# Attention and routed experts on one core: x and output transposed by DMA, x in a ring of five, second attends and scatters moved forward

## The chip, the cores and the metric

The kernel runs on one core of one Trainium2 chip. Five engines work side by side, each through its own instructions in order, and wait for each other on semaphores: TensorE (PE, matmuls), VectorE (DVE), ScalarE (ACT), GpSimd (POOL) and SyncE (SP, which here only issues DMAs). 16 DMA engines move the data. The metric is the device time of one execution in microseconds (us), less is better.

## What is computed

x is [8, 1024, 256] in float32. With a row norm of x, xn, the result is x plus an attention of xn plus a mixture of experts of xn (which itself adds xn):

```
xn = layernorm(x)
Q, K, V = heads(xn@Wq+bq), heads(xn@Wk+bk), heads(xn@Wv+bv)      # 16 heads of 16
Qp, Kp = relu(unit(Q)@proj)+0.1, relu(unit(K)@proj)+0.1          # 64 features, unit: by the vector's norm
out = (Qp @ (Kp.T V)) / (Qp @ sum(Kp)) ; attn = out @ Wo + bo
top 2 of 8 experts per row, capacity 2561, ranks counted over all rows in order
ffn = sum_k gate_k * (silu(xn_row @ w1[e]) @ w2[e]) + xn
result = x + attn + ffn
```

## The kernel before

Every float32 matrix is split into a high and a low float16 part and multiplied in three passes (`PASSES`). The kernel has two stages. **The attention loop** goes over the 8 batches b. One turn (`pe_turn`, `dve_turn`, `act_turn`, `pool_turn`, `sp_turn`, each an order written out by hand for its engine) does the attention of batch b and, woven into it, the preparation ("prep") of batch b+1: the last turn (7) is the "tail" without a preparation. **The expert stage** follows: 71 tiles of 256 gathered rows go through the experts, with POOL's gathers and adding scatters and SP's DMA transposes (`rows_turn`, L429).

A turn, in DVE's order: `choose` (top 2 experts, L1258 MAX8 first); `row_sums(b+1)` (bn_stats L1198, waits for x of batch b+1); `v_over_norm(b, 1)` (L1248 to L1250, waits for POOL's `norm_refine`); `row_factors` (L1206, rsqrt chain); `normalise_rows` (L1216); `place_read`; the copy of the key-value sums kvt (L1385); `q_low` (L1319, low part of the q features); `kv_build`; `constant_part` and four `attend_drain` (L1336) for half 0 of the batch; q_low of half 1; `normalise`, `place` (the slots of each row, L1280 to L1298), `o_low` (L1352); the same for half 1; in between `qk_halves` of b+1 (L1232); `norms` (guess of 1/sqrt, L1238, then POOL refines, L1034 to L1039); `out_drain` (L1363: adds resid).

ACT reads x's high part (`xn_high`), the features (`k_relu` L517, `q_relu` L525), q and k with bias (`qk_read_half`, L505 and L507), v (L547), and makes `resid` (L559) as the last thing of a preparation. SP's `x_load(b+2, half)` waits for `resid_ready` of batch b+1, since resid is made from the same two x buffers. `hi` and `lo` parts of xn and of the attention's output are turned on PE (`x_transpose` L718, `o_transpose` L833; 8 transposes a bank) and copied out of PSUM by ACT (L543, L578). POOL makes low parts (`x_low`, `w_low`), refines norms in 13 steps and scatters 16 sets of 128 records per batch into the slot table (`scatter`, L1046): eight after the last attend, then `norm_refine`, then eight. Each turn also splits one expert's weights (`w_load`, `w_high`, `w_low`, `w_store`). Three small PSUM banks go round in the order of `BODY`: each user waits until the user three before has been read.

## Time and profile before

| | us |
|---|---|
| median of 3 runs | 1437.63 (1431.65 to 1439.33) |
| the profiled execution | 1448.41 |
| its span, first to last instruction | 1446.8 |
| attention loop with its start | about 677 |
| expert stage | about 770 |
| mean granted TensorE clock | 0.912 |

Over the span PE is busy 86%, DVE 55%, ACT 46%, POOL 55%. In a timeline each row is a start, a duration, the engine, the line and the operation with what it writes and reads; in brackets stands how long the engine sat idle before and what released it. "remote" there is a release that the profile can't name. A line with "SPq" is the issue of a DMA.

### The profile page before, as it was taken

How to read it: one execution, taken by the hardware profiler on the slowest of the kernel's cores; microseconds unless marked ns; L12 is line 12 of the kernel's file. 1: busy time of each engine (PE TensorE's matmuls, PEld its weight loads, DVE VectorE, ACT ScalarE, POOL GpSimd, SP SyncE). 2: the span in 40 equal slices, each digit the busy share in tenths (PEclk: the TensorE clock that was granted, in tenths of full speed). 3: DMA queues.
4: the chain of work that ended last, by engine and by line, in shares of the span. 5: the costliest groups of instructions: out<-in, count | busy, mean ns of one | idle time of the engine just before them, and what ended most of it. 6: DMA issues, size and time to landing. Idle time of an engine off the chain costs nothing.

```text
span 1446.8 us, 38172 instructions
## 1 busy us (share of the span) xinstructions
PE 1250.6 (86%) x14334; PEld 997.8 (69%) x14334; DVE 792.5 (55%) x1830; ACT 663.7 (46%) x1140; POOL 802.3 (55%) x804
## 2 busy tenths in 40 slices
PE   4886877878796968644999999999999999999997
PEld 2555554545555545423888888888888888888886
DVE  6676858586767677653433434344444434344442
ACT  3766766666766666631323323232323333232322
POOL 3637382846556473861256656555555556565553
PEclk9798787979797978856999999999999999999999
DMA  2223232322413232504864444444544444344451
GB/s 84 98 73 111 89 118 89 118 89 75 132 45 118 89 105 66 182 25 154 275 180 82 78 77 70 75 75 74 78 75 74 77 77 77 69 77 75 78 78 15
DMA packets 156139, 133.73 MB, mean 92 GB/s; under 512 B 93825, under 2 KB 144258, under 8 KB 154946
## 3 DMA queue, kind: packets, MB, share of 16 engines
q1 hardware_dynamic: 122338, 95.58, 23.2%
q0 software_dynamic: 33632, 35.71, 15.3%
q8 instruction: 129, 2.11, 0.6%
q14 instruction: 40, 0.33, 0.1%
HBM read 61.83 MB, written 52.61 MB: 79 GB/s over the span
## 4 chain that ended last, share of the span: by engine, by line
PE 58%; DVE 18%; issue 7%; DMA 5%; ACT 5%; POOL 5%; SPq 1%; another core or an unknown queue 1%; ACTq 0%; DVEq 0%; POOLq 0%
PE bank L944 26%; PE bank L960 25%; DVE area L1319 4%; DMA area<-in_x_dram 4%; POOL slot_table L1046 2%; DVE area L1198 2%; DVE area L1216 1%; ACT area L559 1%; PE bank L821 1%; DVE area L1187 1%; PE bank L807 1%; ACT area L578 1%; PE bank L728 1%; PE bank L705 1%
## 5 line engine op out<-in xcount | busy, mean ns | idle before, releaser
L944 PE MATMUL bank<-area 128*128 128x256 f16 x3408 | 385.5, 273 | 20.0 <-DMA area<-xg 15.3
L960 PE MATMUL bank<-area 128*128 x3408 | 383.5, 273 | 0.0
L944 PEld LDWEIGHTS bank<-area 128*128 x3408 | 334.1, 98 | 60.4 <-issue 21.1
L1142 POOL DMA_INDIRECT out_dram<-area,mt x142 | 229.6, 1617 | 251.3 <-ACT area L647 221.8
L1468 DVE TENSOR_SCALAR area<-area 128x512 f16<-128x512 f32 x284 | 129.0, 454 | 422.0 <-ACT area L637 390.0
L960 PEld LDWEIGHTS bank<-area 128*128 128x128 f16 x3408 | 333.3, 98 | 38.7
L637 ACT ACTIVATE area<-bank 128x512 f32<-128x512 f32 x284 | 169.6, 598 | 189.3 <-PE bank L944 176.0
L1046 POOL DMA_INDIRECT slot_table<-area x128 | 128.2, 1001 | 149.3 <-PE bank L821 107.3
L647 ACT ACTIVATE area<-bank,mt 128x256 f32<-128x256 f32 x142 | 59.6, 470 | 329.5 <-PE bank L960 324.8
L1470 DVE SCALAR_TENSOR_TENSOR area<-area 128x512 f16<-128x512 f32 x284 | 196.9, 693 | 9.8
L1135 POOL DMA_INDIRECT xg<-xn_split,mt x142 | 143.5, 1010 | 44.7 <-issue 42.7
L765 PE MATMUL bank<-p_hl,area 32*128 32x128 f16 x1536 | 67.8, 258 | 44.9 <-issue 35.2
L1127 POOL DMA_DIRECT2D mt<-slot_table x71 | 54.3, 765 | 77.1 <-issue 77.1
L705 PE MATMUL bank<-area,w_hl 128*128 128x512 f16 x384 | 95.1, 409 | 1.3 <-ACT area L543 1.3
L765 PEld LDWEIGHTS bank<-p_hl,area 32*128 32x128 f16 x1536 | 55.4, 114 | 55.7 <-issue 45.8
L1319 DVE SCALAR_TENSOR_TENSOR area<-bank,area 128x512 f16<-128x512 f32 x128 | 79.5, 682 | 21.1 <-ACT area L525 20.8
L807 PE MATMUL bank<-area,p_hl 32*128 32x512 f16 x384 | 55.6, 497 | 35.5 <-DVE area L1319 35.5
L525 ACT ACTIVATE area<-bank 128x512 f16<-128x512 f32 x128 | 67.6, 598 | 39.8 <-PE bank L807 22.9
L1007 POOL TENSOR_TENSOR area<-area 128x1024 f16<-128x1024 f32 x16 | 35.4, 2211 | 83.9 <-ACT area L537 83.9
L705 PEld LDWEIGHTS bank<-area,w_hl 128*128 128x128 f16 x384 | 40.1, 105 | 50.3 <-issue 14.0
L1002 POOL TENSOR_TENSOR area<-area 128x1024 f16<-128x1024 f32 x32 | 68.0, 2127 | 0.3 <-ACT area L498 0.2
L505 ACT ACTIVATE area<-bank,bqk_w 128x512 f32<-128x512 f32 x64 | 45.4, 709 | 41.1 <-PE bank L705 41.1
(172 smaller groups left out, 1457.7 us busy)
## 6 DMA issues: line engine op xcount, KB each, us to landing
area<-in_w_dram SPq DMA_DIRECT2D x32, 512.0 KB, 5.3
experts_split<-area SPq DMA_DIRECT2D x32, 512.0 KB, 4.3
area<-experts_split SPq DMA_DIRECT2D x8, 2048.0 KB, 8.1
area<-in_x_dram SPq DMA_DIRECT2D x16, 512.0 KB, 6.8
xn_split<-area SPq DMA_DIRECT2D x16, 512.0 KB, 3.0
out_dram<-area SPq DMA_DIRECT2D x32, 256.0 KB
xg<-xn_split,mt POOLq DMA_INDIRECT x142
area<-xg SPq DMA_TRANSPOSE x142
```

Of the source, the lines that this page charges most:

```text
L637: nc.scalar.activation(h32[j].rearrange("p a b -> p (a b)"), big[j][:, :], ACT.Silu, scale=1.0 / R_SCALE).then_inc(mh_silu, 1)
L705: mm = nc.tensor.matmul(big[n][:, :], w_hl[:, wl, k, c0:c0 + P], xT[half][:, xl * KC + k, :], start=(i == 0 and k == 0), stop=(i == 2 and ...
L765: mm = nc.tensor.matmul(big[j][:, c:c + P], k_hl[g // 2][rows_, m, kl, tok:tok + P], p_hl[rows_, pl, m, j * P:(j + 1) * P], start=(i == 0) ...
L807: mm = nc.tensor.matmul(big[j][:, :], p_hl[rows_, pl, m, j * P:(j + 1) * P], q_hl[half][rows_, m, ql, :], start=(i == 0), stop=(i == 2))
L944: mm = nc.tensor.matmul(big[j][:, i2 * TS:(i2 + 1) * TS], we[:, bass.ds(e * EXPERT + (k * 2048 + wl * 1024 + c * P), P)], moe_xT[t % XT][: ...
L960: mm = nc.tensor.matmul(yb[:, a * D:(a + 1) * D], hT[u % 2][:, c, hl, a * P:(a + 1) * P], we[:, bass.ds(e * EXPERT + off, D)], start=(c == ...
L1046: nc.gpsimd.indirect_dma_start(meta, bass.IndirectOffsetOnAxis(slot_i[:, k, t:t + 1], 0), rec[:, k, t, :], None).then_inc(meta_stored, 16)
L1135: nc.gpsimd.indirect_dma_start(xg[:, t % XR, a, :], None, xs, bass.IndirectOffsetOnAxis(mt[:, u % GRP, a, 0:1], 0)).then_inc(rows_in[t % X ...
L1142: nc.gpsimd.indirect_dma_start(orows, bass.IndirectOffsetOnAxis(mt[:, u % GRP, a, 0:1], 0), y_sb[u % 2][:, a, :], None, bounds_check=last_ ...
L1319: v.scalar_tensor_tensor(rq[:, p_, 1, :], big[n % BIG_BANKS][:, :], 0.0, rq[:, p_, 0, :], ALU.max, ALU.subtract).then_inc(qf_split, 1)
L1468: v.tensor_scalar(hT[u % 2][:, 2 * j:2 * j + 2, 0, :], h32[j], H_SCALE, None, ALU.mult).then_inc(mh_step, 1)
L1470: v.scalar_tensor_tensor(hT[u % 2][:, 2 * j:2 * j + 2, 1, :], h32[j], H_SCALE, hT[u % 2][:, 2 * j:2 * j + 2, 0, :], ALU.mult, ALU.subtract ...
```

## The change

- `resid` goes; the rows are overwritten in place (`resid_rows`), in a ring of five half batches of x (`x_in(b, half)`). `x_load(b+2, 0)` is first in `sp_turn`, `x_load(b+2, 1)` waits until out1 of batch b is drained.
- `row_sums` and `row_factors` of batch b+2 are made in turn b, between `out_drain(b, 0)` and `out_drain(b, 1)`.
- xn and the output are transposed by DMA from SP (`x_turn`, `o_turn`, four of [128, 512] float16 each), behind the store and the load of weights; PE's transposes and ACT's copies go. PE and ACT wait for `x_turned` and `o_turned`.
- The second attends come right after the q features of half 1; `place` follows them on DVE, and the 16 scatters go in one piece. nd has two buffers.
- The norms of half 0 are refined on DVE in place of POOL.

The diff, cut to its core:

```diff
 XR = 4
+HALVES = 5
...
-BODY = (attn("rank", "vsum", "kvT") + prep("xT0", "xT1") + attn("cn", "ab0", "ab1", "ab2", "ab3") + prep("xT2", "xT3")
-        + attn("oT0", "oT1", "ab4", "ab5", "ab6", "ab7") + prep("v0", "v1", "nrm0", "v2", "nrmT0", "v3")
-        + attn("out0", "out1", "oT2", "oT3") + prep("v4", "v5") + attn("out2", "out3") + prep("v6", "nrm1", "v7", "nrmT1"))
+BODY = (attn("rank", "vsum", "kvT", "cn", "ab0", "ab1", "ab2", "ab3", "ab4", "ab5", "ab6", "ab7")
+        + prep("v0", "v1", "nrm0", "v2", "nrmT0", "v3") + attn("out0", "out1") + prep("v4", "v5") + attn("out2", "out3")
+        + prep("v6", "nrm1", "v7", "nrmT1"))
...
-        x_in = [view([HT, D], F32) for _ in range(2)]
+        x_half = [view([HT, D], F32) for _ in range(HALVES)]
...
-        resid = view([NT, D], F32)
...
-        nd = view([HT, H, HD + 1], F32)
+        nd = [view([HT, H, HD + 1], F32) for _ in range(2)]
...
+        def x_in(b, half):
+
+            return x_half[(2 * b + half) % HALVES]
...
-            src = xrows[bass.ds(b * S + half * HS, HS), :].rearrange("(t p) d -> p t d", p=P)
-            hold(sp, resid_ready, (b - 1) * 2 + half + 1)
-            sp.dma_start(x_in[half], src).then_inc(x_loaded[half], 16)
+            src = xrows[b * S + half * HS:b * S + half * HS + HS, :].rearrange("(t p) d -> p t d", p=P)
+            n = 2 * b + half - HALVES
+            if n >= 0:
+                wait_read(sp, "attn", f"out{2 * (n % 2) + 1}", n // 2)
+            if b > 0:
+                sp.wait_ge(x_loaded[half], b * 16)
+            sp.dma_start(x_in(b, half), src).then_inc(x_loaded[half], 16)
+
+        def x_turn(sp, b, half):
+
+            if b > 0:
+                sp.wait_ge(prep_filled, nth("prep", f"v{half * HT + HT - 1}", b - 1))
+            sp.wait_ge(xl_split, b * 2 + half + 1)
+            for t in range(HT):
+                sp.dma_start_transpose(xT[half][:, :, t * P:(t + 1) * P],
+                                       xhl[half][:, t].rearrange("p h n -> p (h n)")).then_inc(x_turned[half], 16)
+
+        def o_turn(sp, b, half):
+
+            if half == 1:
+                sp.wait_ge(attn_filled, nth("attn", "out1", b))
+            elif b > 0:
+                sp.wait_ge(attn_filled, nth("attn", "out3", b - 1))
+            sp.wait_ge(o_split, b * 2 + half + 1)
+            for t in range(HT):
+                sp.dma_start_transpose(oT[:, t], o_hl[:, t].rearrange("p h n -> p (h n)")).then_inc(o_turned[half], 16)
 
         def xs_store(sp, b, half):
...
         def sp_turn(sp, b, phase, x_next=True):
             body = phase == "body"
-            if body:
-                xs_store(sp, b + 1, 0)
+            if body and x_next:
+                x_load(sp, b + 2, 0)
             w_store(sp, b, 0)
             w_load(sp, b, 2)
             if body:
-                xs_store(sp, b + 1, 1)
+                x_turn(sp, b + 1, 0)
+                xs_store(sp, b + 1, 0)
             w_store(sp, b, 1)
             w_load(sp, b, 3)
+            if body:
+                x_turn(sp, b + 1, 1)
+                xs_store(sp, b + 1, 1)
+            o_turn(sp, b, 0)
+            w_store(sp, b, 2)
+            if body:
+                w_load(sp, b + 1, 0)
             out_store(sp, b, 0)
+            o_turn(sp, b, 1)
             out_store(sp, b, 1)
-            w_store(sp, b, 2)
-            if body:
-                w_load(sp, b + 1, 0)
             if body and x_next:
-                x_load(sp, b + 2, 0)
+                x_load(sp, b + 2, 1)
             out_store(sp, b, 2)
             out_store(sp, b, 3)
-            if body and x_next:
-                x_load(sp, b + 2, 1)
             w_store(sp, b, 3)
...
             sp.wait_ge(consts_ready, 1)
             for half in range(2):
+                x_load(sp, 1, half)
                 xs_store(sp, 0, half)
-                x_load(sp, 1, half)
                 w_load(sp, 0, half)
...
         def resid_rows(act, b, half):
 
             act.wait_ge(resid_scales, b * 2 + 2)
-            if b > 0:
-                wait_read(act, "attn", f"out{2 * half + 1}", b - 1)
+            x_rows = x_in(b, half)
             for t in range(HT):
                 n = half * HT + t
-                ins = nc.scalar.activation(resid[:, n, :], x_in[half][:, t, :], ACT.Identity, bias=shift[:, n:n + 1],
+                ins = nc.scalar.activation(x_rows[:, t, :], x_rows[:, t, :], ACT.Identity, bias=shift[:, n:n + 1],
                                            scale=grow[:, n:n + 1])
             ins.then_inc(resid_ready, 1)
...
             act.wait_ge(o_ready, b * 2 + half + 1)
-            nc.scalar.copy(o_hl.rearrange("p t l (h d) -> p l t h d", h=H)[:, 0], nd[:, :, :, 0:HD]).then_inc(o_high, 1)
-
-        def oT_copy(act, phase, b, half):
-            for j in range(2):
-                src = f16(take(act, phase, "attn", f"oT{2 * half + j}", b)).rearrange("p (t c q) -> p t c q", t=2, c=4)
-                nc.scalar.copy(oT[:, 2 * j:2 * j + 2], src).then_inc(attn_taken, 1)
+            if half == 1:
+                act.wait_ge(o_turned[0], (b + 1) * 16 * HT)
+            elif b > 0:
+                act.wait_ge(o_turned[1], b * 16 * HT)
+            nc.scalar.copy(o_hl.rearrange("p t l (h d) -> p l t h d", h=H)[:, 0], nd[half][:, :, :, 0:HD]).then_inc(o_high, 1)
...
             q_relu(act, b, 1)
             if body:
-                xT_copy(act, phase, b + 1, 1)
-                qk_read_half(act, b + 1, 0, 0, 1)
+                qk_read_half(act, b + 1, 0, 0, 2)
             o_hi(act, b, 0)
-            if body:
-                qk_read_half(act, b + 1, 0, 1, 2)
-            oT_copy(act, phase, b, 0)
             if body:
                 qk_read_half(act, b + 1, 0, 2, 4)
                 v_copy(act, phase, b + 1, 0)
                 v_copy(act, phase, b + 1, 1)
                 squares_copy(act, phase, b + 1, 0)
                 v_copy(act, phase, b + 1, 2)
+                v_copy(act, phase, b + 1, 3)
             o_hi(act, b, 1)
             if body:
-                v_copy(act, phase, b + 1, 3)
-            if body:
+                resid_rows(act, b + 1, 0)
+                qk_read_half(act, b + 1, 1, 0, 4)
                 w_high(act, b, 3)
-                qk_read_half(act, b + 1, 1, 0, 2)
-            oT_copy(act, phase, b, 1)
+                resid_rows(act, b + 1, 1)
             if body:
                 v_copy(act, phase, b + 1, HT)
                 v_copy(act, phase, b + 1, HT + 1)
-                qk_read_half(act, b + 1, 1, 2, 4)
                 last_copies(act, phase, b + 1)
...
             q_features(pe, b, 1, 1)
-            if body:
-                x_transpose(pe, phase, b + 1, 1)
-                qk_project(pe, b + 1, 0, False)
-            o_transpose(pe, phase, b, 0)
             for t in range(HT, NT):
                 attend(pe, phase, b, t)
             if body:
+                qk_project(pe, b + 1, 0, False)
                 v_and_squares(pe, phase, b + 1, 0)
+            if body:
+                qk_project(pe, b + 1, 1, False)
             o_project(pe, phase, b, 0)
-            if body:
-                qk_project(pe, b + 1, 1, False)
-            o_transpose(pe, phase, b, 1)
             if body:
                 v_and_squares(pe, phase, b + 1, 1, attended=b)
...
             w_low(pool, b, 2)
-            pool.wait_ge(attn_filled, nth("attn", f"ab{NT - 1}", b))
-            scatter(pool, b, 0, 8)
-            norm_refine(pool, b + 1, 0)
-            scatter(pool, b, 8, 16)
+            scatter(pool, b)
             w_low(pool, b, 3)
             norm_refine(pool, b + 1, 1)
             v_total(pool, b + 1)
...
-            rsqrt_guess(chp, ny, nsq, nu, ready=norm_guess)
+            if half == 1:
+                rsqrt_guess(chp, ny, nsq, nu, ready=norm_guess)
+                return
+            rsqrt_guess(chp, ny, nsq, nu)
+            for step in range(3):
+                chp.link(v.tensor_tensor(nu, nsq, ny, ALU.mult))
+                chp.link(v.scalar_tensor_tensor(ny, nu, -0.5, ny, ALU.mult, ALU.mult) if step == 2 else
+                         v.scalar_tensor_tensor(nu, nu, -0.5, ny, ALU.mult, ALU.mult))
+                chp.link(v.scalar_tensor_tensor(ny, ny, 1.5, nu, ALU.add, ALU.mult) if step == 2 else
+                         v.scalar_tensor_tensor(ny, nu, 1.5, ny, ALU.add, ALU.mult))
+            chp.link(v.tensor_scalar(norm[:, 0], ny, 1e-8 * W_SCALE, None, ALU.add))
...
         def dve_turn(dve, b, phase, first=False):
             body = phase == "body"
-            cha.start(dve, b)
             choose(dve, b)
-            if body:
-                chp.start(dve, b + 1)
-                row_sums(dve, b + 1)
             if not body:
                 place_read(dve, phase, b)
                 place(dve, b, first)
             v_over_norm(dve, b, 1, cha)
             if body:
-                row_factors(dve)
                 normalise_rows(dve, b + 1, 0)
-            if body:
                 place_read(dve, phase, b)
             else:
                 tile_table(dve)
@@ -1391,32 +1375,32 @@
             constant_part(dve, b, 0)
             for t in range(HT):
                 attend_drain(dve, phase, b, t)
-            q_low(dve, b, 1, 0, PAIRS)
-            normalise(dve, b, 0)
-            if body:
-                place(dve, b, first)
-                qk_halves(dve, b + 1, 0, 0, 1)
-            o_low(dve, b, 0)
+            q_low(dve, b, 1, 0, 4)
             constant_part(dve, b, 1)
+            q_low(dve, b, 1, 4, PAIRS)
             for t in range(HT, NT):
                 attend_drain(dve, phase, b, t)
             if body:
-                qk_halves(dve, b + 1, 0, 1, 4)
+                place(dve, b, first)
+            normalise(dve, b, 0)
+            if body:
+                qk_halves(dve, b + 1, 0, 0, 2)
+            o_low(dve, b, 0)
             normalise(dve, b, 1)
             if body:
+                qk_halves(dve, b + 1, 0, 2, 4)
                 norms(dve, phase, b + 1, 0)
+                v_over_norm(dve, b + 1, 0, chp)
             o_low(dve, b, 1)
+            if body:
+                qk_halves(dve, b + 1, 1, 0, 4)
             out_drain(dve, phase, b, 0, first)
-            if body:
-                qk_halves(dve, b + 1, 1, 0, 2)
-                v_over_norm(dve, b + 1, 0, chp)
-                qk_halves(dve, b + 1, 1, 2, 3)
+            if body and b + 2 < B:
+                row_sums(dve, b + 2)
+                row_factors(dve, b + 2)
             out_drain(dve, phase, b, 1, first)
             if body:
-                qk_halves(dve, b + 1, 1, 3, 4)
                 norms(dve, phase, b + 1, 1)
-                chp.end()
-            cha.end()
...
-            for half in range(2):
-                qk_halves(dve, 0, half)
-                if half == 1:
-                    v_over_norm(dve, 0, 0, chp)
-                norms(dve, "first", 0, half)
-            chp.end()
+            qk_halves(dve, 0, 0)
+            norms(dve, "first", 0, 0)
+            v_over_norm(dve, 0, 0, chp)
+            qk_halves(dve, 0, 1)
+            norms(dve, "first", 0, 1)
+            row_sums(dve, 1)
+            row_factors(dve, 1)
```

Beside it `row_sums(1)` and `row_factors(1)` stand ahead of the first turn, `row_factors` waits for `resid_ready` of the batch before, `xn_high` waits for `x_turned`, PE's `o_project` waits for `o_turned`, and `bo_row`, `bo_hl` and `vtmp` share other buffers.

## Rows read from the trace of the kernel before

**Rows 1.** Windows by stage: us; per engine busy us (xinstructions); PEclk, DMA share, GB/s
```profile
199.00:277.00 78.00, 62.89 (x940) 41.12 (x938) 56.73 (x153) 53.69 (x89) 45.77 (x54) 0.82 0.31 96
720.00:1440.00 720.00, 713.47 (x6533) 638.65 (x6530) 309.75 (x540) 218.69 (x407) 406.85 (x337) 1.00 0.45 79
```

**Rows 2.** Timeline of DVE, turn 2: start, us, engine, line, operation [idle before]
```profile
119.88 0.64 DVE L1258 MAX8 area<-area 128x8 f32<-128x8 f32 x8
...
198.19 0.64 DVE L1258 MAX8 area<-area 128x8 f32<-128x8 f32 x8
...
207.84 2.71 DVE L1198 BATCH_NORM_STATS2 area<-area 128x6 f32<-128x256 f32 x8 [2.89 <-DMA area<-in_x_dram]
...
264.12 0.69 DVE L1363 SCALAR_TENSOR_TENSOR area<-bank,area 128x512 f32<-128x512 f32 x1 [0.83 <-remote]
...
276.48 0.64 DVE L1258 MAX8 area<-area 128x8 f32<-128x8 f32 x8
```

**Rows 3.** Timeline of SP's queue, turn 2: issues of DMAs
```profile
200.97 0.38 SPq L386 DMA_DIRECT2D area<-in_x_dram  x1
```

**Rows 4.** Timeline of ACT, turn 2
```profile
203.32 2.06 ACT L517 ACTIVATE area<-bank 128x512 f32<-128x512 f32 x4 [2.38 <-remote]
...
223.03 2.06 ACT L525 ACTIVATE area<-bank 128x512 f16<-128x512 f32 x4
```

**Rows 5.** Timeline of PE, turn 2 and tail turn
```profile
218.90 0.65 PE L790 MATMUL bank<-xg,area 128*32 128x64 f32 x32
...
274.86 0.63 PE L744 MATMUL bank<-ident,area 128*128 128x128 f32 x4
...
613.64 1.93 PE L790 MATMUL bank<-area 128*32 128x64 f32 x64 [6.40 <-DVE area L1250]
```

**Rows 6.** Windows of one engine alone, DVE four times, then POOL
```profile
221.96:264.81 42.85, 33.05 (x75) 0.80 0.24 80
243.22:246.14 2.92, 2.54 (x17) 1.00 0.00 0
6.16:12.16 6.00, 5.52 (x31) 1.00 0.69 195
269.72:271.56 1.84, 1.80 (x4) 1.00 0.01 1
...
203.86:210.97 7.11, 6.04 (x16) 0.65 0.77 261
```

**Rows 7.** Groups by line in turn 2: busy us, mean ns, idle before
```profile
L578 ACT COPY area<-bank 128x1024 f16<-128x1024 f16 x4 | 3.9, 1028 | 2.0 <-PE bank L833 2.0
...
L1280 DVE TENSOR_TENSOR area<-area 128x128 f32<-128x128 f32 x1 | 0.3, 285 | 0.0
```

**Rows 8.** Transposes of the expert stage: by line, SP's timeline, a window of half a us
```profile
L429 SPq DMA_TRANSPOSE area<-xg x142: 1189/1262/2782, 677.6 to 1412.5; - x142
...
802.21 2.50 SPq L429 DMA_TRANSPOSE area<-xg  x2
...
805.00:805.50 0.50, 0.50 (x7) 0.44 (x6) 0.00 (x0) 0.50 (x1) 0.50 (x1) 1.00 0.79 156
```

**Rows 9.** Landing times: L386's loads of x, page part 6, chain of waits
```profile
DMA to landing us min/median/max: 6.5/6.8/8.1
...
xn_split<-area SPq DMA_DIRECT2D x16, 512.0 KB, 3.0
...
1.44 4.62 DMA area<-in_x_dram
```

**Rows 10.** Timelines around scatters: POOL and DVE in turn 2, PE in the tail
```profile
261.55 0.96 POOL L1046 DMA_INDIRECT slot_table<-area  x1 [0.30 <-issue]
...
262.60 0.69 DVE L1363 SCALAR_TENSOR_TENSOR area<-bank,area 128x512 f32<-128x512 f32 x1 [3.58 <-remote]
...
629.29 0.23 PE L821 MATMUL bank<-area 128*128 128x34 f16 x2 [1.23 <-issue]
...
640.67 0.66 PE L821 MATMUL bank<-area 128*128 128x34 f16 x17 [1.23 <-issue]
```

More of the change, by code:

```diff
@@ L289, in moe_attention @@
         xn_ready = sem("xn_ready")
+        x_turned = [sem(f"x_turned{i}") for i in range(2)]
         xs_stored = [sem(f"xs_stored{i}") for i in range(2)]
@@ L315, in moe_attention @@
         o_split = sem("o_split")
+        o_turned = [sem(f"o_turned{i}") for i in range(2)]
         out_stored = [sem(f"out_stored{i}") for i in range(2)]
@@ L452, in _ @@
             sp.dma_start(xs[N:N + P, :], zero_rows).then_inc(zero_stored, 16)
+            for half in range(2):
+                x_turn(sp, 0, half)
             sp.wait_ge(consts_ready, 1)
             for half in range(2):
+                x_load(sp, 1, half)
                 xs_store(sp, 0, half)
-                x_load(sp, 1, half)
                 w_load(sp, 0, half)
@@ L668, in _ @@
             last_copies(act, "first", 0)
+            for half in range(2):
+                resid_rows(act, 0, half)
             act_turn(act, 0, "body", first=True)
@@ L823, in attend @@
             mm.then_inc(attn_filled, 1)
-        def o_transpose(pe, phase, b, half):
-            for j in range(2):
-                dst = f16(small_ap(phase, "attn", f"oT{2 * half + j}", b, pe)).rearrange("p (t c q) -> p t c q", t=2, c=4)
-                if j == 0:
-                    pe.wait_ge(o_split, b * 2 + half + 1)
-                for tl in range(2):
-                    for hl in range(2):
-                        for m in range(KC):
-                            mm = nc.tensor.transpose(dst[:, tl, hl * KC + m, :],
-                                                     o_hl[:, 2 * j + tl, hl, m * P:(m + 1) * P], ident16[:, :])
-                mm.then_inc(attn_filled, 1)
         def o_project(pe, phase, b, half):
@@ L1021, in norm_refine @@
             g = nc.gpsimd
-            steps = [(b * 2 + half) * 13]
+            steps = [b * 13]
             def link(ins, apart=False):
@@ L1030, in link @@
                     pool.wait_ge(pool_norm, steps[0])
-            hold(pool, norm_guess, b * 2 + half + 1)
+            hold(pool, norm_guess, b + 1)
             for _ in range(3):
@@ L1039, in norm_refine, with scatter @@
             g.tensor_scalar(norm[:, half], nu, 1e-8 * W_SCALE, None, ALU.add).then_inc(norm_ready, 1)
-        def scatter(pool, b, n0=0, n1=TOPK * NT):
+        def scatter(pool, b):
             pool.wait_ge(slots_ready, b + 1)
-            for n in range(n0, n1):
+            for n in range(TOPK * NT):
                 k, t = n // NT, n % NT
@@ L1197, in row_sums, with row_factors @@
             for t in range(NT):
-                chp.step(v.bn_stats(bn[:, t, :], x_in[t // HT][:, t % HT, :]))
-            hold(dve, dve_prep, chp.base + chp.n)
+                chp.step(v.bn_stats(bn[:, t, :], x_in(b, t // HT)[:, t % HT, :]))
+            chp.wait()
             for t in range(NT):
                 chp.step(v.bn_aggr(mv[:, t, :], bn[:, t, :]))
-        def row_factors(dve):
+        def row_factors(dve, b):
             chp.wait()
             chp.link(v.tensor_scalar(va, mv[:, :, 1], 1e-5, None, ALU.add))
+            if b > 0:
+                dve.wait_ge(resid_ready, b * 2)
             rsqrt(chp, vy, va, vu)
```

94 lines of the change are left out of this document (33 added, 61 removed).

## The prediction, made before the changed kernel was run

> **What bounds the kernel now.** I read the stage table first [rows 1]. TensorE (PE) is busy in 713.5 of 720 us of the expert stage, which the change doesn't touch; in a turn of the attention loop no engine is full (PE 62.9, VectorE (DVE) 56.7, ScalarE (ACT) 53.7, GpSimd (POOL) 45.8 of 78 us). So a turn is bound by a chain of hand-offs, and I looked next at what DVE does in one [rows 2]. A turn runs from one `choose` (MAX8, 198.19) to the next (276.48): 78.3 us. I write times in a turn as c+t, c being that start. DVE waits 2.9 us for the DMA of x, at c+9.6 it begins the statistics; v over norm, row factors and the first rows follow, and it copies the key-value sums (L1385) only at c+23.8 [rows 6]. The load of x was issued at 200.97, since SyncE's queue (SP) had waited until ACT had written resid [rows 3]. ACT's first k relu starts at c+5.1, its first q relu at c+24.8, after rows that DVE normalised late [rows 4], though PE had ended its sums at 219.55, c+21.4 [rows 5]. Then comes DVE's long stretch to the end of the drain of out1, 264.81, c+66.6; and 11.7 us from there to the next choose [rows 2].
>
> **The front of a turn.** The change loads x and makes its statistics a turn ahead, and takes resid off the turn's last place on ACT. So ACT can begin its k relus at about c+0.1. From that relu to PE's last sum it was 203.32 to 219.55, 16.2 us [rows 4, 5]. v over norm of half 1 needs POOL's 13 steps, 7.1 us [rows 6], which now start at c (POOL's scatters are over by then, below); with its own work of 1.8 and a copy held up behind POOL it ends near c+10.3, and PE wants it at about c+12. I put L1385 at c+16.2 (bounds 15.5 and 17.5): a gain of 7.6 us. This is all that the early x gives.
>
> **The transposes.** Removed per turn: 64 transposes on PE and 8 copies on ACT of 1.02 us [rows 7]. The x ones lay beside DVE's q splits: no gain. For o, PE's first bank and ACT's two copies were the path, about 2.7 us (0.6+2x1.03) from o_low to oT. Added are 16 transposes on SP. The expert stage shows the same [128x512] f16 form: 142 of them, 1.19 to 2.78 us of SP each, a pair in 2.50, and the data of a pair's second moving until about 805.5, 2.0 us after its issue at 803.5 [rows 8]. So a half of four holds SP 5.0 us and is there 3.75+2.1 = 5.9 us after its first issue. The same rows bound SP's part by 4.8 (4 at 1.19) and 11 us (4 at 2.78); I take the pair, which is two in a row. Against 2.7 us that is 3.2 later for o, and **whatever stands behind them in SP's queue waits 5 us more**.
> The Trainium skill (Advanced Engine Details and Errata, section X-Bar Transpose (TRN2)) says that transposing DMAs on this chip are as fast as regular ones. The rows disagree for this form: a 512 KB store lands in 3.0 us [rows 9], a transposed half in 5.9. What the rule would give is one of the rivals.
>
> **From L1385 to out1's drain.** DVE was busy in 33.05 of 42.85 us of this stretch [rows 6]; 4.4 of the rest were late signals for the two drains of out (one in rows 10). New in it: ten links of norm refinement, taken from POOL, on 128x128 elements, nearest row L1280 with 0.285 [rows 7], so with hand-offs 3.1 us; v over norm of half 0, 1.8 [rows 6], and two qk halves of about 0.74, which stood behind out1's drain before. That is 39.5 us of work, some 41 with the hundredths between chained steps. The waits come from a ladder, in which each step starts when its engine and its inputs are free (durations as in before): q relus 16, attend drains 0 to 3 end 28.8, q splits of half 1 with constant part 1 in their gap end 34.4, PE's second attends and their drains 38.1, place (2.9 [rows 6]) 41.0, normalise 0 43.0, two qk halves, o_low 0 45.7. SP transposes o half 0 until 51.6; only then may ACT overwrite o_hl (52.7), write resid half 0 (2.0 us) and read q and k of half 1 in 4 pairs of 1.3 us, until 59.9. DVE meanwhile has qk halves, normalise 1, norms, refinement, v over norm until 55.8, o_low 1 57.0; its last qk half waits for ACT, 60.6, and out1 is drained at c+62.0, where it was c+66.6. So 45.8 us, and 4.6 us of the gain are left here.
>
> **From there to the next choose.** This term decides. `x_load(b+2,1)` takes the ring's buffer that out1's drain frees, and stands on SP behind `o_turn(b,1)` and a store; `row_sums(b+2)` stands on DVE right behind that drain and ahead of `out_drain(b,1)`. So: SP's store of out0 61.75, four transposes 66.7, a store 67.1, the x load. It lands 4.6 us later at the least (the chain's first load, from 1.44) or 6.8 (median of 14, 6.5 to 8.1) [rows 9]; I take 5.5, nearer the first, since little else is in flight: 72.6. Statistics and row factors, 6.0 us where POOL is still [rows 6]: 78.6. out2 drained 79.3. PE's square sums wait for exactly that bank (three small banks in turn): 1.06, ACT's copy 0.6, the transpose 0.63 (rows 5 has the last), DVE's 0.8, with 0.2 of hand-offs: choose at **c+82.6**, against 78.3. POOL's 16 scatters at 1.27 run from 41.0 to 61.3, under cover. PE idles from about 72 on. **A wait chain of 20.6 us stands where 11.7 stood.**
>
> **Sum.** Five turns (1 to 5) of +4.3: +21.5. The first: PE's first projection waits 5.9 us for four transposes instead of about 3 (+3); statistics of batch 1 (6.0) now stand ahead of the first choose and hold up the gates and v over norm: out1 near 112.8 instead of 108.2, the next choose at 112.8+20.6 = 133.3 instead of 119.9 [rows 2]: +13.4. Turn 6 has no statistics: o half 1 is there at 67.6, out2 drained 70.1, choose 75.4: -2.9. Tail turn: PE's wait of 6.4 us for v over norm [rows 5] and some 2 us of late relus go, -8.4; two o halves with 3.2 more each, less what the earlier attends give back, +5.4: -3.0. Together +29 us. Against the profiled execution, 1448.4, that is 1477; it lies 10.8 above the median of the runs shown, and I set the difference on the median: 1437.6+29 = **1466.6 us**. Every bound low: a turn of 77.0 (no idle on DVE beyond its 41, load 4.6), first turn +8, turn 6 -8, tail -8: -14.5, 1423. Every bound high: a turn of 86.6 (load 6.8, transposes at 1.5, front 17.5): +60, 1498.
>
> **Rivals.** (1) Not slower: the ladder is too pessimistic, and DVE runs from L1385 to out1 with little idle. It decides where front, stretch and tail sum below 78.3, so at a stretch under 42.3 us with the load at 4.7 (mine is 45.8); halfway the sum is about 1437, at the end 1423. For it: DVE's work alone allows it, and a wait of known length stands only at the load. Against it: in the trace DVE idles 9.8 us in this stretch [rows 6], and o_hl adds a wait. Chance 0.22. A variant: four transposes take SP and the DMA engines no longer than one plain DMA of 512 KB (0.38 on SP [rows 3], 3.0 to land [rows 9]); SP would be free 4.6 us earlier, the turn 78.0 and the sum about 1434; 142 rows speak against it, 0.02. It is what the page named above would give.
> (2) Much slower: signals freeze while POOL issues scatters. In the trace DVE's drain of out0 starts as POOL's eighth scatter in a row ends, 3.6 us after DVE was free; and in the tail turn, under 16 in a row, PE's attends come one or two per 1.2 us until 640.67, then 17 at once [rows 10]. The change puts 16 in a row into every turn, c+41 to c+61, over square sums, norms, and q and k of half 1. If nrmT0, due at 48.9, reaches DVE only at 61.3, about 11.7 us later, each of seven turns grows by as much: 1466.6+82 = 1549. Against it: the tail's freeze alone is some 12 us and the runs without a recording are 10.8 shorter, as if the freeze were the recording's. 0.18, partial freezes included.
> The Trainium skill (SBUF — State Buffer, section SBUF: two separate sides, the box on the "DVE blocks DMA" trap) warns that DVE work on the port it shares with GpSimd keeps POOL from writing descriptors, and refinement now runs on DVE during scatters. The rows don't show it: scatters keep 0.96+0.30 us beside DVE's work [rows 10], so nothing is charged.
> (3) My forecast, slower by 12 to 60 us: 0.58.
>
> **Chances.** A difference within 0.5% (7 us) is what a measurement can't tell from none. Rival 1 with its variant (0.24) split into faster 0.10 and same 0.14; slower is 0.76. The range leaves out most of rival 2 and the low end of rival 1: 1430 to 1512.
>
> **What would show it.** In the changed kernel: DVE waiting 8 to 11 us per turn at bn_stats for the DMA of x, with PE idle beside the end of it; the copy of the key-value sums near c+16; out1 drained near c+62; on SP four transposes of 1.25 us ahead of the x load. A DVE wait of 5 us or more for nrmT0 would be rival 2. I am wrong if the statistics start without a wait, or if a turn takes 78 us or less.

## The result and the profile after

The changed kernel takes 1497.11 us (median of 4, 1496.20 to 1500.55) against 1438.07 us (4 runs, 1431.65 to 1439.33) for before: ratio 1.0427, interval 1.0403 to 1.0450, slower by 59 us where 29 were forecast. Its profiled execution took 1496.2 us, span 1494.5.

Windows of after: turn 2, turn 6 (which has no statistics), the expert stage; columns as in [rows 1]:

```profile
219.16:302.54 83.38, 56.03 (x863) 34.27 (x858) 59.15 (x164) 46.48 (x81) 41.37 (x39) 0.80 0.43 117
...
560.03:641.92 81.89, 56.86 (x885) 34.10 (x879) 53.77 (x134) 46.47 (x81) 41.66 (x39) 0.79 0.43 102
...
772.00:1494.00 722.00, 711.33 (x6511) 636.57 (x6509) 307.17 (x536) 218.08 (x406) 404.79 (x336) 1.00 0.45 78
```

The expert stage takes 761.2 us from its first matmul on, for 760.4. PE does less in a turn (56.0 us against 62.9 [rows 1]), yet a turn is 5 us longer. Timeline of DVE, turn 2 of after, the lines that answer to [rows 2]:

```profile
219.16 0.64 DVE L1249 MAX8 area<-area 128x8 f32<-128x8 f32 x8
...
234.74 0.41 DVE L1369 COPY area<-bank 128x256 f32<-128x256 f32 x1
...
280.54 1.28 DVE L1353 SCALAR_TENSOR_TENSOR area<-bank,area 128x512 f32<-128x512 f32 x2
...
291.68 2.71 DVE L1176 BATCH_NORM_STATS2 area<-area 128x6 f32<-128x256 f32 x8 [9.86 <-DMA area<-in_x_dram]
...
297.67 1.28 DVE L1353 SCALAR_TENSOR_TENSOR area<-bank,area 128x512 f32<-128x512 f32 x2
...
301.81 0.29 DVE L1218 COPY area<-bank 128x128 f32<-128x128 f32 x1 [2.86 <-PE bank L747]
```

The copy of the key-value sums stands at c+15.6 (before: c+23.8), out1 is drained at c+62.7, and then DVE does nothing for 9.9 us. SyncE's queue says what it waits for:

```profile
265.73 5.13 SPq L414 DMA_TRANSPOSE area<-area  x4
...
281.25 0.39 SPq L424 DMA_DIRECT2D out_dram<-area  x1
281.74 5.14 SPq L414 DMA_TRANSPOSE area<-area  x4
286.92 0.58 SPq L424 DMA_DIRECT2D out_dram<-area  x1
287.60 0.41 SPq L395 DMA_DIRECT2D area<-in_x_dram  x1
```

Store, four transposes, store, then the load of x at c+68.4, which lands 4.1 us later. PE in the same stretch:

```profile
288.23 0.58 PE L835 MATMUL bank<-area 2*128 2x512 f16 x1 [6.10 <-DMA area<-area]
288.74 2.74 PE L839 MATMUL bank<-wo_hl,area 128*128 128x256 f16 x12
...
298.41 1.08 PE L740 MATMUL bank<-area,hsel 128*32 128x512 f32 x8 [4.05 <-DVE area L1353]
```

It waits for the transposed o half, 6.5 us behind its first issue, and then for DVE's drain of out2. The same twelve matmuls took 1.48 us before; windows of PE alone, first after, during DVE's wait, then before, from out1's drain to choose:

```profile
281.82:291.68 9.86, 3.76 (x17) 0.52 0.61 160
```
```profile
264.81:276.48 11.67, 10.44 (x114) 1.00 0.36 120
```

The granted clock is 1.00 up to about c+63, where PE's six matmuls end that stand between a wait of 2.6 us and one of 6.1, and 0.50 (the level of 1.2 GHz) from c+64 to c+73, so also for the twelve matmuls of 2.74 us. Over the window that makes 0.52. In before's window, with PE busy in 10.4 of 11.7 us, it stays at 1.00.

Turns are 79.6, 82.8, 83.4, 85.2, 86.8, 85.6 and 81.9 us. They differ mostly by when o half 0 is transposed. ACT's second o_hi, which waits for it, in turns 2 and 4, and SP's four issues in turn 4:

```profile
272.21 1.04 ACT L602 CAST area<-area 128x1024 f16<-128x1024 f32 x1 [2.46 <-DMA area<-area]
...
443.59 1.04 ACT L602 CAST area<-area 128x1024 f16<-128x1024 f32 x1 [5.37 <-DMA area<-area]
```
```profile
434.22 6.96 SPq L414 DMA_TRANSPOSE area<-area  x4
```

From first issue to landing: 6.5 us in turn 2, 9.4 in turn 4, where out1's drain ends at c+65.5 instead of c+62.7. GpSimd's 16 scatters run beside it, from c+42 to c+63.

### The profile page after: what moved, and what is told of

Its sections match the earlier page's. It is cut to its first block, busy times and chain, and to the rows that moved or that the text cites. A ratio compares the mean times of both kernels' runs of the same rounds, so it can differ in the third digit from the quotient of the medians.

```text
span 1494.5 us, 37183 instructions
## 1 busy us (share of the span) xinstructions
PE 1221.0 (82%) x13822; PEld 958.3 (64%) x13822; DVE 819.8 (55%) x1910; ACT 605.0 (40%) x1076; POOL 762.5 (51%) x690
## 4 chain that ended last, share of the span: by engine, by line
PE 52%; DMA 2%; DVE 1%; issue 1%; SPq 1%; POOL 0%; ACT 0%; POOLq 0%
PE bank L930 25%; PE bank L946 25%; DMA area<-experts_split 1%; PE bank L839 1%; SPq L414 1%; DMA area<-area 1%; PE bank L810 0%; PE bank L824 0%; PE bank L793 0%; POOL out_dram L1120 0%; DVE area L1310 0%; PE bank L835 0%; DVE area L1241 0%; DMA experts_split<-area 0%; DMA out_dram<-area,mt 0%
## 5 line engine op out<-in xcount | busy, mean ns | idle before, releaser
L946 PEld LDWEIGHTS bank<-area 128*128 128x128 f16 x3408 | 333.4, 98 | 38.8 <-issue 0.2
L1030 POOL DMA_INDIRECT slot_table<-area x128 | 138.1, 1079 | 123.0 <-DVE dump_f L1289 80.3
L664 ACT ACTIVATE area<-bank,mt 128x256 f32<-128x256 f32 x142 | 59.6, 471 | 329.5 <-PE bank L946 329.5
L1105 POOL DMA_DIRECT2D mt<-slot_table x71 | 54.0, 761 | 76.2 <-issue 76.2
L1018 POOL TENSOR_TENSOR area<-area 128x128 f32<-128x128 f32 x24 | 11.0, 456 | 147.0 <-DVE area L1155 145.8
L721 PEld LDWEIGHTS bank<-area,w_hl 128*128 128x128 f16 x384 | 39.2, 104 | 72.2 <-issue 35.6
L731 PE MATMUL bank<-w_hl,area 128*128 128x264 f16 x384 | 58.1, 297 | 26.5 <-DVE area L1353 26.5
L824 PEld LDWEIGHTS bank<-area 128*128 128x128 f16 x1536 | 45.2, 106 | 51.0 <-issue 33.9
L824 PE MATMUL bank<-area 128*128 128x34 f16 x1536 | 47.3, 191 | 31.8 <-issue 22.9
L731 PEld LDWEIGHTS bank<-w_hl,area 128*128 128x128 f16 x384 | 37.6, 103 | 53.3 <-DVE area L1353 31.0
```

The lines of the kernel that those rows point to most:

```text
L721: mm = nc.tensor.matmul(big[n][:, :], w_hl[:, wl, k, c0:c0 + P], xT[half][:, xl * KC + k, :], start=(i == 0 and k == 0), stop=(i == 2 and ...
L731: mm = nc.tensor.matmul(dst[:, 0:D + E], xT[half][:, xl * KC + k, tl * P:(tl + 1) * P], w_hl[:, wl, k, 2 * D:], start=(i == 0 and k == 0), ...
L824: mm = nc.tensor.matmul(dst[:, p_ * KVW:(p_ + 1) * KVW], rq[:, p_, rl, tl * P:(tl + 1) * P], kv_hl[:, kl, p_, :], start=(i == 0), stop=(i ...
L946: mm = nc.tensor.matmul(yb[:, a * D:(a + 1) * D], hT[u % 2][:, c, hl, a * P:(a + 1) * P], we[:, bass.ds(e * EXPERT + off, D)], start=(c == ...
L1030: nc.gpsimd.indirect_dma_start(meta, bass.IndirectOffsetOnAxis(slot_i[:, k, t:t + 1], 0), rec[:, k, t, :], None).then_inc(meta_stored, 16)
```

## The experiments

The chips on which these ran differ, so ratios to before on the same chip are given. DMA transposes are in none of these kernels. The expert stage's are plain copies of the same tiles, and those of a turn are stood in for by plain copies (**copies**) or made by PE as before (**on PE**). So the price of the transposing DMA itself is bracketed, not measured apart. The plain copies leave out the turning: the experts, and where the turn has copies too also q, k, v and the routing, work on unturned rows, with the same numbers of matmuls, copies and bytes. c is a turn's choose, as in the prediction.

**1. The control, and how the time of a turn follows the queue.** In before, `dma_start_transpose(moe_xT..., xg...)` became `dma_start`.

> The kernel before with the expert stage's 142 transposing DMAs made plain copies of the same tiles (what is left out: the turning of the gathered rows; the experts multiply unturned rows). Every other kernel of the study has this too. It is the control for it: TensorE bounds that stage (713.5 of 720 us busy), so every theory expects the time of before, 1438 us, within 5 us, and turns of the attention loop of 78.3 us.

1432.3 us, ratio 0.9960 (0.9945 to 0.9975); turns of 78.4 us. Of the 5 us less, 3.2 lie in the expert stage (757.2 for 760.4 us in the profiles).

Then after, with one or three copies for each transpose (the three move a half, a quarter and a quarter of the tile):

```
-  sp.dma_start_transpose(oT[:, t], o_hl[:, t]...)
+  for c0, c1 in O_PARTS: sp.dma_start(oT[:, t, c0:c1], src[:, c0:c1])     (x the same)
```

> The kernel after with each of its 16 transposing DMAs a turn replaced by three plain copies that together move the same [128x512] f16 tile (left out: the turning of x and o, so q, k, v and the routing are made from unturned rows; the counts of matmuls, copies and bytes are the same). Three issues of about 0.42 us with gaps of 0.05 hold SyncE's queue 5.6 us for a half where four transposes held it 5.1. Theory (what the transposes cost is their time in the queue and the landing behind it): 1497 us within 8, with the wait of 9 to 10.5 us for x at bn_stats and turns of 82 to 87 us. Rival (it is the transposing itself, by the DMA engines' own work, that stretches everything else): 1480 us or less.

1530.8 us, ratio 1.0645 (1.0627 to 1.0662): both sides missed, since twelve issues hold SP longer than I had reckoned. SP, then DVE, in turn 2:

```profile
296.36 7.55 SPq L419 DMA_DIRECT2D area<-area  x12
303.95 0.59 SPq L429 DMA_DIRECT2D out_dram<-area  x1
304.64 0.41 SPq L397 DMA_DIRECT2D area<-in_x_dram  x1
```
```profile
308.79 2.71 DVE L1181 BATCH_NORM_STATS2 area<-area 128x6 f32<-128x256 f32 x8 [12.35 <-DMA area<-in_x_dram]
```

> As the kernel with three copies, but one plain copy for each transposing DMA: a half of four holds SyncE's queue 1.9 us. My forecast's variant said 1434 us for this. With the measured turns of 84.7 us: x is loaded 3.5 us earlier at the turn's end, the second o_hi of ScalarE comes 3 us earlier and out1's drain 1 to 2.5 us, so turns of 79 to 80 us and 1460 us, 1450 to 1467. Rival (the statistics' wait stays whatever the queue does, since out1's drain frees the buffer at c+62): 1475 or more. Rival (transposes are the whole loss): 1440 or less.

1458.7 us, ratio 1.0134 (1.0107 to 1.0160), as expected from after's turns. SP is held for 2.40 us, DVE waits 8.67:

```profile
272.00 2.40 SPq L419 DMA_DIRECT2D area<-area  x4
```
```profile
280.75 2.71 DVE L1181 BATCH_NORM_STATS2 area<-area 128x6 f32<-128x256 f32 x8 [8.67 <-DMA area<-in_x_dram]
```

Means of turns 1 to 5 against SP's hold by a half of o: 80.9 us at 2.4, 84.7 at 5.1 (after), 89.4 at 7.6. That is 1.4 and 1.9 us of turn for one of queue: a half in the queue is paid behind out1's drain, and the other one partly before it, through ACT's o_hi. A line between the two kernels of plain copies gives 85.3 at 5.1 us (an estimate), so after's transposes cost about what plain copies with their hold would.

**2. Both transposes on PE**, with ident16, the banks and ACT's copies of before; ring, statistics, attends and scatters as in after.

> The kernel after with both transposes back on TensorE and their copies on ScalarE, as in before, and the expert stage's 142 transposing DMAs made plain copies (left out: the turning of the gathered rows). What is left of the change is the ring of five, the early statistics, the early second attends and the 16 scatters in a row. Theory (ring and order are sound, the DMA transposes and what they do to SyncE's queue cost all): the load of x goes out as out1 is drained, near c+61, lands at c+65.5, statistics until c+71.5, out2 drained c+72, choose c+76: turns of 76 to 77 us, the first +5, turn 6 and the tail -10 together: 1423 us, 1415 to 1435. Rival (statistics between the two drains cost even with a free queue, because x still lands 4.4 us after the drain that frees its buffer): turns of 79 us or more, 1440 or more.

1443.5 us, ratio 1.0056 (1.0039 to 1.0073); against the control, 11 us slower (14 by the two ratios). The rival won, my theory missed by 20 us. Turn 2:

```profile
275.18 1.28 DVE L1379 SCALAR_TENSOR_TENSOR area<-bank,area 128x512 f32<-128x512 f32 x2
...
281.93 2.71 DVE L1202 BATCH_NORM_STATS2 area<-area 128x6 f32<-128x256 f32 x8 [5.47 <-DMA area<-in_x_dram]
```

With an empty queue DVE still waits, since the buffer is freed by the very drain that stands ahead of the statistics; turn 2 has the shortest of these waits, in turns 1 to 5 they are 5.5 to 8.2 us, 6.7 on average. Turns with them take 80.0 us, turn 6 without takes 72.8 (74.4 when the same kernel ran again). Against the control this kernel is at 1.0056/0.9960 = 1.010; what is left to after's 1.0427 is a factor of 1.033, and that is what transposing by DMA costs over transposing on PE.

**3. Take the wait away.** `HALVES = 6`, and both `x_load(b+2)` at the head of `sp_turn`; statistics stay. It ran twice, on two chips, the second time beside its base.

> The kernel with the transposes on TensorE (turned_by_pe: 1443.5 us, turns of 80.0), with six half buffers in the ring and both loads of batch b+2 at the head of turn b. Theory (what is lost against before is the wait for the load of x, 5.5 us of DVE in each turn with statistics): bn_stats starts as out1 is drained, c+62.5, ends with the factors c+68.5, out2 and out3 drained at c+70.5, choose at c+74.6: six turns of 5.4 us less, 1411 us, 1405 to 1420. Rival (statistics between the two drains cost by their own 6 us, wherever x is: turn 6 without them took 72.8): 1425 to 1435. Rival (the DMAs moved to the head of the turn get in the way there): 1438 or more.

> The kernel with both transposes on TensorE once more, on one chip with the three below. On the chip where before takes 1437 us and no wait is put down as remote it was 1443.5 (ratio 1.0056). If this chip is like that, the same ratio. If it is like the other one (before 1445 us, remote waits of 3 to 5 us for PE's and DVE's signals until the last of 16 scatters has gone at c+64): out1 is drained at c+66 instead of c+62 and the tail turn is 13 us or more longer, 1443.5 + 6*3 + 15 = 1475 us, ratio about 1.02.

> Ring of six and both loads of x at the head of the turn, transposes on TensorE. Theory (the wait of 5.5 us for x goes): 25 to 32 us less than turned_by_pe_2 on the same chip, whichever chip it is. Rival (DMAs or the statistics' own 6 us hold the end): within 8 us of it.

On the first chip (before: 1445 us) it took 1457.1 us, ratio 1.0080 (1.0049 to 1.0111): the theory's range is missed, and the last rival's, in which this lies, is met for another reason (below). On the second (before: 1436) the base took 1445.7 (1.0055, 1.0036 to 1.0074) and this 1410.5, ratio 0.9821 (0.9804 to 0.9838), the 1411 expected, and 35 us below its base where 25 to 32 were: the wait that goes is longer than the 5.5 us reckoned with. It is 1.4% below the control, whose expert stage has plain copies too, so it beats before as well as after. There, turn 4, DVE goes on without a wait, and the turn takes 73.6 us (turns 1 to 5: 74.4 on average):

```profile
411.49 1.28 DVE L1379 SCALAR_TENSOR_TENSOR area<-bank,area 128x512 f32<-128x512 f32 x2
412.69 2.70 DVE L1202 BATCH_NORM_STATS2 area<-area 128x6 f32<-128x256 f32 x8
```

On the first chip, the same turn, DVE between the drains of out0 and out1 and ACT before the copy of o's transposed half 1:

```profile
432.69 0.69 DVE L1379 SCALAR_TENSOR_TENSOR area<-bank,area 128x512 f32<-128x512 f32 x1 [3.43 <-remote]
```
```profile
432.78 1.93 ACT L585 COPY area<-bank 128x1024 f16<-128x1024 f16 x2 [4.90 <-remote]
```

Both wait until c+65.6, as GpSimd's last scatter (issued at c+63.4) has gone. Such waits for a remote signal stood in the profile of before too [rows 10], and in none of after, of the control or of the other kernels on chips where before takes 1436 to 1438 us. Their place is that of my rival 2. Four kernels ran on that chip, all with such waits, and the same four elsewhere without any: so whether they come depends on the chip. On which chip the profile of before was taken isn't on record; its 1448.4 us lies among the 1441 to 1449 that before takes on this one. What after would take there isn't known.

**4. Only the order in SP's queue.** One copy for each transpose, `x_load(b+2,1)` ahead of `o_turn(b,1)`.

> The kernel with one plain copy for each transposing DMA, and x_load(b+2,1) ahead of o_turn(b,1) in SyncE's queue. Theory (each us that the load of x waits in the queue is a us of the turn): the load goes out at c+61.5 instead of c+64.2, bn_stats starts at c+67 instead of c+69.8, and the copies of o half 1, 0.5 us later, still land before the statistics end at c+73: 2.5 us less in each of six turns, 1443 us, 1440 to 1448. Rival (o half 1, now behind the load, becomes the bound): 1455 or more.

> One plain copy for each transposing DMA, once more. Where no remote waits stand 1458.7 (ratio 1.0134); on a chip with them 3 to 4 us more in each turn and 15 in the tail, 1495 us, ratio 1.035.

> The same with x_load(b+2,1) ahead of o_turn(b,1). Theory (each us of the load's wait in the queue is a us of the turn): 10 to 16 us less than one_copy_for_one_2 on the same chip. Rival (o half 1, which now waits for out1's drain as well, takes the load's place as the bound): within 5 us of it. The first look had it 24 us above one_copy_for_one, but on another chip; if that is the edit and not the chip, it is again 15 us or more above.

The first run was on the chip with remote waits and gave 1482.8 us, ratio 1.0257 (1.0224 to 1.0289). On the other: base 1458.7 (1.0151, 1.0133 to 1.0168), edit 1440.9, ratio 1.0051 (1.0022 to 1.0079): inside the first range, and somewhat more than the 10 to 16 us of the second. 18 us for two lines exchanged: the load goes out at c+60.8 instead of c+63.8, and DVE waits 5.44 instead of 8.5:

```profile
267.32 0.38 SPq L397 DMA_DIRECT2D area<-in_x_dram  x1
267.80 2.48 SPq L419 DMA_DIRECT2D area<-area  x4
```
```profile
272.73 2.71 DVE L1181 BATCH_NORM_STATS2 area<-area 128x6 f32<-128x256 f32 x8 [5.44 <-DMA area<-in_x_dram]
```

**5. The wait away, the queue still slow.** Three copies, ring of six, loads at the head of the turn.

> The kernel with three plain copies for each transposing DMA (1530.8 us, ratio 1.0645; turns of 89.4, DVE waits 12.3 us for x), with the ring of six and both loads of x at the head of the turn. Theory (with so slow a queue, o half 1 is the next bound, so only part of the wait comes back): the statistics end at c+72, PE still gets o half 1 at c+74.5, so the turn ends as its turn 6 without statistics, 84.6: six turns of 4.7 us less, 1503 us, ratio 1.045 (1.040 to 1.050). Rival (the wait comes back whole, 12 us a turn): 1460 us or less.

1503.3 us, ratio 1.0479 (1.0452 to 1.0506). DVE's 12.35 us of waiting are gone, but turns fall only from 89.4 to 84.6: the next bound is o half 1, as PE's projection ends:

```profile
288.43 2.70 DVE L1180 BATCH_NORM_STATS2 area<-area 128x6 f32<-128x256 f32 x8
...
300.66 0.69 DVE L1357 SCALAR_TENSOR_TENSOR area<-bank,area 128x512 f32<-128x512 f32 x1 [6.17 <-PE bank L843]
```

By the same reading the wait of 9.9 us in after is worth what turn 6 shows, 84.7-81.9 = 2.8 us; but there out1 is drained at c+65.8, in turns 1 to 5 at c+63.8 on average, so it may be up to 4.8. Both are estimates, no run took the wait out of after. The 9.1 us from turn 6 to the 72.8 of turn 6 on PE (7.5 to its second run) are the transposes'.

**6. The statistics elsewhere**: `row_sums`, `row_factors` behind the next turn's choose; transposes on PE, ring of five.

> The kernel with the transposes on TensorE and row_sums and row_factors taken from between the drains and put right behind the next turn's choose. There DVE waits 4.1 us for GpSimd (v over norm), so 6 us of statistics push the copy of the key-value sums from c+15.6 to c+17.6 to c+19. Theory: the end of a turn is that of turn 6, so a turn takes 72.8+2 to 3.5 = 75 to 76.3 us against 80.0, six of them: 1415 to 1425 us. Rival (DVE's work is the bound, so it does not matter where the statistics stand): 1438 or more.

> The kernel with the transposes on TensorE and the statistics behind the next turn's choose, once more. Its first look showed the row factors, chained operations on [128x8], taking 1.1 to 2.3 us each beside GpSimd's norm refinement where they take 0.17 to 0.31 alone, and the copy of the key-value sums at c+22 instead of c+15.6. Theory: a turn is that of turn 6 without statistics and 6.4 us more, 72.8+6.4 = 79.2 against 80.0: on a chip without remote waits 1438 us, ratio 1.002 (0.999 to 1.005); with them 1485 again, ratio 1.027.

1485.1 us, ratio 1.0269 (1.0234 to 1.0303), on the chip with remote waits; 1435.3, ratio 0.9990 (0.9974 to 1.0005), on the other. Turns take 78.3 us: the first expectation, 75 to 76.3, failed, and only 8 us are gained on the base; the second, 1438 us, holds within 3 us. The place was free only in name. DVE, then GpSimd beside it, operations of DVE that take 0.17 us between the drains:

```profile
210.24 2.30 DVE L1191 TENSOR_TENSOR area<-area 128x8 f32<-128x8 f32 x1
...
214.76 2.04 DVE L1193 SCALAR_TENSOR_TENSOR area<-area 128x8 f32<-128x8 f32 x1
...
224.42 0.42 DVE L1398 COPY area<-bank 128x256 f32<-128x256 f32 x1 [1.95 <-PE bank L798]
```
```profile
209.64 0.54 POOL L1047 TENSOR_SCALAR area<-area 128x128 f32<-128x128 f32 x1
210.16 2.35 POOL L1020 TENSOR_TENSOR area<-area 128x1024 f32<-128x1024 f32 x1
...
214.66 2.12 POOL L1010 TENSOR_TENSOR area<-area 128x1024 f16<-128x1024 f32 x1
```

The expectation put this down to the norm refinement. The rows say otherwise: the refinement ends at 210.2 (L1047 is its last step), and DVE's operations on [128x8] beside it take 0.17 to 0.23 us. The two slow ones start just after a large subtraction or addition of GpSimd (`v_total`, L1020, and `w_low`, L1010) and end with it, 212.54 for 212.51 and 216.80 for 216.78. The key-value sums are copied at c+21.5 instead of c+15.6.

**7. Two scatters instead of 16** in each turn but the last, one copy for each transpose.

> The kernel with one plain copy for each transposing DMA (1458.7 us, turns of 80.9) with 2 of 16 scatters in each turn but the last (left out too: 14 of 16 stores of a turn into the slot table). Theory (16 scatters in a row cost next to nothing): 1454 to 1460 us; of single waits only that of ScalarE's second o_hi in turn 6 (4.9 us) goes. Rival (scatters hold up signals or the transfers beside them in every turn): 3 us or more less a turn, 1438 or less.

> One plain copy for each transposing DMA, 2 of 16 scatters in each turn but the last, once more (base: 1458.7 us, ratio 1.0134 and 1.0151). Its first look had turns of 79.1 against 80.9 and 73.7 against 78.9 in turn 6, but a tail turn of 108 us with all 16 scatters on the chip with remote waits. Theory: without such waits the tail is 86 us again, so 5*1.8+5 = 14 us less than the base: 1444 us, ratio 1.004 (1.001 to 1.007). Rival (scatters cost nothing where nothing is put down as remote): ratio 1.011 or more.

On the chip with remote waits 1465.6 us, ratio 1.0141 (1.0111 to 1.0172). Its turns are those of the other chip, 79.1 us, with no remote wait before the tail, so there it is the row of scatters that brings the waits. Its tail takes 108 us for 87.6. Under the tail's 16 scatters (619.3 to 639.3) DVE's copy of the key-value sums waits 16.6 us, and under the expert stage's first eight gathers (from 660.3) PE's attends crawl from 660.30 to 671.64 as in [rows 10]:

```profile
642.01 0.42 DVE L1375 COPY area<-bank 128x256 f32<-128x256 f32 x1 [16.64 <-remote]
```

On the other chip 1443.9, ratio 1.0066 (1.0044 to 1.0087): the first expectation (scatters cost next to nothing) fails, the second holds, with turns of 79.1 for 80.9 and 73.9 for 78.9. The load of x lands 4.3 instead of 5.5 us after its issue, and ACT's wait for the first half in turn 6 goes. So 14 scatters more a turn cost 15 us there in all (10 to 12 by the ratios) with no signal held up; what shows is that DMAs beside them land later.

## Why the prediction was wrong, step by step

**What bounds, and the sign: right.** The term called decisive was: out1 drained c+62.0, load issued 67.1, statistics at 72.6, choose 82.6; turn 2 shows 62.7, 68.4, 72.5 and 83.4. The 72.5 is in part luck: the load goes out 1.3 us late and lands 1.4 us sooner than reckoned. And turn 2 is the second shortest of turns 1 to 5, which take 84.7 on average. The front (15.6 to 16.4, forecast 16.2) is right.

**Wrong by 30 us** are four terms of the sum: turns 1 to 5 by 10.6, turn 6 by 4.8, the first turn by 3.1, the tail and what it was compared with by 11.3. 1497 lies in the range, but near its upper end.

1. *Turns 1 to 5*: +32.1, forecast +21.5. "So a half of four holds SP 5.0 us and is there ... 5.9 us after its first issue": the hold is 5.13, the landing 6.5 to 9.4. It was read from pairs of the expert stage; here half 1, issued as the last scatters go, lands in 6.5 us each time, and half 0, beside the scatters, in 6.5 to 9.4. ACT's second o_hi starts at c+53.0 to c+55.9 instead of 51.6, and from the copy of the key-value sums to the end of out1's drain it is 48.0 us on average, not 45.8. Experiment 7 shows the scatters' part, on copies. From out1's drain to the issue of the load it is 5.8 us instead of 5.1, and from the start of out2's drain to choose 5.1 on average instead of 4.0: PE's lower clock, with 1.1 to 1.9 us for the square sums, up to 1.50 for 0.85 for v's six matmuls behind them (not in my chain) and up to 1.06 for 0.63 for the transposes. In turn 1, where these ran at the full clock, it is 4.0. I had priced them at full clock and written "PE idles from about 72 on" without asking what idling does to the clock. Landing of x went the other way, 4.1 for 5.5. A gain of 4.6 us up to out1's drain was also read off late signals: the control, without them, drains out1 in turn 2 at c+63.4 and not 66.6, and has 15.4 us from there to choose, not 11.7. This leaves the sum alone, which counts from c.

2. *Turn 6*: "o half 1 is there at 67.6, out2 drained 70.1, choose 75.4". PE starts it at c+72.2, out2 and out3 are drained at c+76.2 and c+78.8, choose is at c+81.9: +1.9 for -2.9. Transposes again (four issues of 7.45 us for half 0, then 6.5 to land half 1) and the lower clock. Without them this turn takes 72.8.

3. *The first turn*: +16.5, forecast +13.4. The statistics of batch 1 stand ahead of the bias's last split, and that one, L1510, took 2.44 us against 0.63 before, while PE's first key-value sums waited for it. As in experiment 6 it lasts until an addition of GpSimd ends. After, DVE, GpSimd, PE:

```profile
54.47 2.44 DVE L1510 TENSOR_TENSOR area<-area 1x256 f16<-1x256 f32 x1
```
```profile
54.27 2.36 POOL L996 TENSOR_TENSOR area<-area 128x1024 f32<-128x1024 f32 x1
```
```profile
56.97 1.93 PE L793 MATMUL bank<-area 128*32 128x64 f32 x64 [3.54 <-DVE area L1510]
```

4. *The tail and the baseline*: "I set the difference on the median". This was the largest slip. From choose 7 to the first expert matmul after takes 91.4 us: against before's profile (94.9) that is -3.5, as forecast (-3.0). But in that execution PE's attends crawl for 14.7 us, 626.52 to 641.26 [rows 10 has two of them], which the control and after don't do. PE in the tail, control:

```profile
625.53 2.20 PE L821 MATMUL bank<-area 128*128 128x34 f16 x72 [1.16 <-ACT area L597]
```

The control's tail is 83.1 us; against it the term is +8.3. PE's wait of 6.4 us for v over norm, which was to go, is 2.69 in the control and 3.73 in after, and the two halves of o come one after the other, 7.1 and 6.5 us from first issue to PE's projection, where PE's own transposes (experiment 2) take 2.2 and 1.8. I saw the stall, saw that the profile lay 10.8 us above the median, wrote "as if the freeze were the recording's", and still took the tail's gain from the stalled record and the base from runs without it. Sum as measured in the profiles: 16.5+32.1+1.9+8.3+0.8 (expert stage) = 59.6, for 59.0.

**Rival 1 and its variant**: turns would have had to be 78 us or less. One copy for a transpose goes 2.7 of the variant's 4.6 us (2.4 us a half), and the time was 1458.7, not 1434; how much of that is the queue's rest and how much the four slips is not shown. The Trainium skill (Advanced Engine Details and Errata, section X-Bar Transpose (TRN2)) says that a transposing DMA is as fast as a regular one. The traces contradict it for this form: four hold SP for 5.14 us and are there 6.5 us after the first issue, four plain ones of the same tile 2.40 and 4.6.

**Rival 2**: absent from after's profile, so its 1549 us didn't come; the mechanism exists, on a chip where it cost the kernel with the ring of six 47 us (1457 for 1410.5) and before 8. The argument against it, that it was the recording's, was wrong: all seven runs of before there take 1441 us or more, and the profiles taken on three other chips show no such wait.

**What the change is made of**, from the profiles, against the control: with everything but the DMA transposes, first choose +9.7, turn 0 +2.5, turns 1 to 5 +1.6 each, turn 6 -5.7, tail -3.1. The transposes by DMA add to that 1.1, 3.6, 4.7 each, 9.1 and 11.3, and 4.8 in the expert stage, where before has them too.

## What to carry to other kernels

When a load's buffer is freed by the operation just ahead of its consumer, its latency and all that stands before it in the queue are a wait; one more buffer (4 KB a partition) with the load issued early took 35 us off (1445.7 to 1410.5). An item moved onto a queue costs its hold for each dependent item behind it, and its landing if that feeds the chain: here 1.4 to 1.9 us of turn for each us that a half held the queue. Before a difference is set on a median, look for stalls that the profile has and the runs of the median need not have, and cost each stage against one without them.

## What the chip showed unasked

- Whether signals stall beside GpSimd's scatters and gathers changed with the chip: not on three chips where before takes 1436 to 1438 us, 3 to 5 us at several places of a turn on the one where it takes 1445. The kernel with the ring of six, which has hand-offs beside 16 scatters in a row, loses the more: +3.3% against before's +0.6%.
- Twelve plain copies of a half or a quarter of a tile hold SP 7.6 us, 0.63 each, and four whole ones 2.40, 0.60 each: between these, the number of DMAs counts and not their size. A transposing one holds it 1.28.
- DVE operations on [128x8] took up to 2.3 us, 0.17 otherwise, when they started beside a GpSimd operation on [128x1024], and ended with it.
- While PE waited 6.1 us its clock was at the lower level (0.50), and it stayed there for the twelve matmuls that followed: 2.74 us for 1.48.
